# A second-layer mask added by GpSimd, head pairs in the third layer, and a new order of steps, in a four-layer graph kernel

## What is computed

```
x = layernorm(x + L0(x, adj))    # additive attention, leaky relu, softmax masked where adj == 0
x = layernorm(x + L1(x, adj))    # logits Ax^T + Ay + x M x^T, leaky relu, masked where adj <= 0, softmax, elu
x = layernorm(x + L2(x, adj))    # four heads of 32, masked where adj == 0 and off the diagonal, relu
x = layernorm(x + L3(x, adj))    # relation 1: onehot(adj) @ ((xW + b) * sigmoid(xWg + bg)), relu
```

## Time and profile before

| | us |
|---|---|
| median of 3 runs | 483.58 |
| the profiled execution, its own time | 484.45 |
| its span in the profile | 482.7 |
| TensorE matmul busy in the span | 451.3 (93%) |
| VectorE, ScalarE, GpSimd busy | 421.6, 418.1, 308.0 |

### The profile page before, as it was taken

How to read it: one execution, slowest core, us unless ns; L and a number is a source line. 1 busy time by engine, 2 the same in 40 slices (tenths; PEclk the granted TensorE clock), 3 DMA queues, 4 the chain that set the end, 5 groups by cost and what they waited for, 6 DMA issues and landing times. The chain is left out here.

```text
span 482.7 us, 13808 instructions
## 1 busy us (share of the span) xinstructions
PE 451.3 (93%) x3785; PEld 387.5 (80%) x3785; DVE 421.6 (87%) x1637; ACT 418.1 (87%) x1233; POOL 308.0 (64%) x671
## 2 busy tenths in 40 slices
PE   5878899999999999999999999999999999998862
PEld 5666787888889988888888988888888889886642
DVE  4478999999999999999999999999999999878662
ACT  3468999999999999999999999999999999988720
POOL 1245446787767667688767777777776777765441
PEclk9999999999999999999999999999999999999995
DMA  6443233334443333333344433333443321120011
GB/s 203 107 110 67 43 70 80 82 77 98 96 101 97 84 74 75 91 94 91 98 99 100 96 73 78 76 97 87 98 97 87 70 46 34 35 45 24 23 33 46
DMA packets 59942, 38.39 MB, mean 80 GB/s; under 512 B 11225, under 2 KB 55897, under 8 KB 59866
## 3 DMA queue, kind: packets, MB, share of 16 engines
q1 hardware_dynamic: 59866, 37.50, 32.1%
HBM read 25.24 MB, written 8.45 MB: 70 GB/s over the span
## 5 line engine op out<-in xcount | busy, mean ns | idle before, releaser
L1271 POOL TENSOR_SCALAR x<-y,minus_mean,rstd 128x128 f32<-128x128 f32 x244 | 121.7, 508 | 21.8 <-issue 19.4
L839 ACT ACTIVATE p<-p,nmax 128x256 f32<-128x256 f32 x256 | 127.2, 512 | 0.6 <-DVE nmax L1044 0.6
L1246 POOL TENSOR_SCALAR ve<-stats 128x2 f32<-128x2 f32 x128 | 30.6, 239 | 134.6 <-DVE stats L948 129.6
L1253 POOL TENSOR_TENSOR rstd<-ve,minus_half 128x2 f32<-128x2 f32 x128 | 104.3, 815 | 0.0
L1044 DVE CUSTOM_DVE_ANT_0 p<-ps,neg 128x256 f32<-128x256 f32 x256 | 90.8, 421 | 13.2 <-PE ps L607 13.2
L848 ACT COPY p2T<-ps 128x512 f32<-128x512 f32 x128 | 72.8, 607 | 0.1
L618 PE MATMUL ps<-ident,p 128*128 128x128 f32 x512 | 66.9, 273 | 1.5 <-issue 1.1
L618 PEld LDWEIGHTS ps<-ident,p 128*128 128x128 f32 x512 | 57.9, 141 | 2.8 <-issue 2.2
L948 DVE BATCH_NORM_STATS2 stats<-y 128x6 f32<-128x256 f32 x128 | 54.0, 422 | 1.4
L839 ACT ACTIVATION_READ_ACCUMULATOR p<-p,nmax 128x1 f32 x256 | 51.8, 202 | 0.0
L752 ACT COPY xT<-ps 128x256 f32<-128x256 f32 x96 | 36.4, 379 | 15.8 <-PE ps L479 15.7
(11 more groups left out here) (134 smaller groups left out, 1114.8 us busy)
## 6 DMA issues: line engine op xcount, KB each, us to landing
adj_in<-in_adj_dram SPq DMA_DIRECT2D x32, 256.0 KB, 4.3
s2row<-s_rows SPq DMA_DIRECT2D x29, 256.0 KB, 4.0
xT<-in_xT_dram SPq DMA_DIRECT2D x32, 128.0 KB, 4.3
x_in<-in_x_dram SPq DMA_DIRECT2D x32, 128.0 KB, 5.3
x_aside<-x SPq DMA_DIRECT2D x32, 128.0 KB, 3.6
out_dram<-x SPq DMA_DIRECT2D x32, 128.0 KB, 6.3
rs_row<-rs_turned SPq DMA_DIRECT2D x58, 64.0 KB
s_rows<-xw SPq DMA_DIRECT2D x29, 2.0 KB, 4.5
```

Of the source, the lines that this page charges most:

```text
L839: last = nc.scalar.activation(p2(n)[:, k, a, :], p2(n)[:, k, a, :], ACT.Exp, bias=nmax2(n)[:, k, a:a + 1], scale=-1.0, accum_out=sum2(n)[: ...
L1253: nc.gpsimd.tensor_tensor(rstd[layer](n), ve[layer](n), minus_half[:, :], ALU.pow)\
L1271: last = nc.gpsimd.tensor_scalar(dst[:, k, 0:D], y_t[layer](n)[:, k, :], minus_mean[layer](n)[:, k:k + 1], rstd[layer](n)[:, k:k + 1], ALU ...
```

## The change

Five things are changed together.

1. **L1 mask.** `relu1` now writes relu(z) times 4. A new GpSimd step `rmask1` adds the mask (now -9e15 / 0.2) to it. `e1` reads z from PSUM and this tile, and scales by -0.2. `lk1` is gone. The bank of `z1` is released by `e1` rather than by `lk1`.
2. **Head pairs in L2.** `e2`, `exp2` and `pT2` work on a row tile and a pair of heads, with semaphores for each pair. The number of instructions that compute is the same. Two banks of `sc2` are released when the first pair is read.
3. **Weights.** ACT issues the loads of `l1_w` and `l3_w` at its start; SP issues `l2_w`, `bias_rows` and `bo_row`, and does so ahead of the first `xT`.
4. **The end.** SP reads the flag before it waits for the last stores. The flag's three steps are moved forward. Some semaphores are shared to make room.
5. **Order.** Every place in `PLAN` is new, and `xT0` has four buffers instead of two.

```diff
-    "sc2": [("a", "e2a_ready", "e2b_ready")] * HEADS,
+    "sc2": [("a", f"e2a{a // 2}_ready", f"e2b{a // 2}_ready") for a in range(HEADS)],
...
-    "z1": [("b", "leaky_ready")],
+    "z1": [("b", "e1_ready")],
...
-    "tensor": [("proj0", 7293), ("s2_rows", 9289), ("prep_a", 9914), ("prep_c", 10981), ("pT0", 11117),
+    "tensor": [("proj0", 7882), ("s2_rows", 8921), ("prep_a", 9172), ("pT0", 11350), ("prep_c", 11355),
...
-            (l1_w[:, :], t["l1_w"]), (l2_w[:, :], t["l2_w"]), (l3_w[:, :], t["l3_w"]),
+            (l2_w[:, :], t["l2_w"]),
...
+        act_loads = [(l1_w[:, :], t["l1_w"]), (l3_w[:, :], t["l3_w"])]
...
+            flag = flag_value(sp)
             for s in range(RING["x4"]):
                 sp.wait_ge(sem(f"stored{s}"), 16 * len(range(s, B, RING["x4"])))
...
-            with if_relations(sp):
+            with sp.If(flag != 0):
...
-            def pT2(k, j, n):
+            def pT2(k, pair, n):
...
-                pe.wait_ge(sem(f"p_ready2{'ab'[k]}"), n + 1)
-                for a in range(HEADS):
-                    last = pe.transpose(o[:, a * P:(a + 1) * P], p2(n)[:, k, a, j * P:(j + 1) * P], ident[:, :])
+                pe.wait_ge(sem(f"p_ready2{'ab'[k]}{pair}"), n + 1)
+                for a in range(2):
+                    for j in range(T):
+                        last = pe.transpose(o[:, (a * T + j) * P:(a * T + j + 1) * P],
+                                            p2(n)[:, k, 2 * pair + a, j * P:(j + 1) * P], ident[:, :])
...
-                nc.scalar.activation(relu(n).rearrange("p t n -> p (t n)"), bank("z1", n), ACT.Copy,
-                                     scale=SLOPE).then_inc(sem("relu_ready"), 1)
+                nc.scalar.activation(relu(n).rearrange("p t n -> p (t n)"), bank("z1", n), ACT.Relu,
+                                     scale=(1.0 - SLOPE) / SLOPE).then_inc(sem("relu_ready"), 1)
...
-            def lk1(n):
...
             def e1(n):
-                dve.wait_ge(sem("leaky_ready"), n + 1)
-                dve.wait_ge(sem("neg1_ready"), n + 1)
+                dve.wait_ge(sem("rmask_ready"), n + 1)
                 free(dve, "p1", n, "pT_ps1")
-                for k in range(T):
-                    last = nc.vector.tensor_tensor_reduce(p1(n)[:, k, :], relu(n)[:, k, :], neg1(n)[:, k, :],
-                                                          -1.0, HIGHEST, ALU.add, ALU.min, nmax1(n)[:, k:k + 1])
+                o = bank("z1", n)
+                for k in range(T):
+                    last = nc.vector.tensor_tensor_reduce(p1(n)[:, k, :], o[:, k * N:(k + 1) * N], relu(n)[:, k, :],
+                                                          -SLOPE, HIGHEST, ALU.add, ALU.min, nmax1(n)[:, k:k + 1])
...
+            def rmask1(n):
+                pool.wait_ge(sem("neg1_ready"), n + 1)
+                pool.wait_ge(sem("relu_ready"), n + 1)
+                nc.gpsimd.tensor_tensor(relu(n), relu(n), neg1(n), ALU.add).then_inc(sem("rmask_ready"), 1)
```

More of the change, by code:

```diff
@@ L26 @@
 PLAN = {
-    "sync": [("ld_xT", 5924), ("ld_w", 7384), ("ld_adj", 7643), ("s2_out", 7682), ("s2_in", 8068), ("ld_x", 9856),
-        ("rs_in", 14874), ("aside", 17166), ("store", 18875)],
[5 rows of a table removed]
-        ("flag", 24911)],
-    "scalar": [("c_proj0", 7629), ("c_s2", 9333), ("c_prep_a", 9758), ("exp0", 10865), ("c_prep_c", 10970),
-        ("c_pT0", 11102), ("c_prep_d", 11926), ("c_xT1", 12167), ("c_tT", 12280), ("c_prep_b", 12346),
[12 rows of a table removed]
+    "sync": [("ld_w", -5093), ("ld_xT", 5803), ("ld_adj", 7317), ("s2_out", 8417), ("s2_in", 8928), ("ld_x", 9412),
+        ("rs_in", 15164), ("aside", 16727), ("store", 19522)],
[5 rows of a table added]
+        ("flag", 15769)],
+    "scalar": [("c_proj0", 8057), ("c_s2", 9237), ("c_prep_a", 10886), ("exp0", 11179), ("c_pT0", 11325),
+        ("c_prep_c", 11483), ("c_prep_b", 11609), ("c_prep_d", 11760), ("c_xT1", 12179), ("c_tT", 12195),
[9 rows of a table added]
+        ("flag_b", 15926), ("flag_a", 15780)],
+    "gpsimd": [("var0", 11818), ("rsq0", 11976), ("norm0", 12052), ("neg2", 12054), ("rmask1", 12530),
+        ("var1", 13523), ("rsq1", 13554), ("norm1", 13669), ("var2", 16156), ("rsq2", 16377), ("norm2", 16445),
+        ("var3", 18688), ("rsq3", 18724), ("norm3", 19112)],
 }
 RING = {
[1 row of a table removed]
[1 row of a table added]
     "x1": 3, "xT1": 2, "tT": 2, "xw1": 3, "relu": 2, "p1": 2, "p1T": 2, "h": 2, "hexp": 2,
@@ L317, in build, with flag_value @@
         rel_biases = ((t["L3_gnn_b_fwd"], t["L3_gnn_bg_fwd"]), (t["L3_gnn_b_bwd"], t["L3_gnn_bg_bwd"]))
+        def flag_value(engine):
+            engine.wait_ge(sem("flag_ready"), 1)
+            return engine.value_load(excess_flag[0:1, 0:1], min_val=0, max_val=1)
         def if_relations(engine):
-            engine.wait_ge(sem("flag_ready"), 1)
-            flag = engine.value_load(excess_flag[0:1, 0:1], min_val=0, max_val=1)
-            return engine.If(flag != 0)
+            return engine.If(flag_value(engine) != 0)
         wait_registers = {}
@@ L610, in sc2 @@
                             last.then_inc(sem("sc_ps"), 1)
-            def pT2(k, j, n):
-                step = f"pT2{'ab'[k]}{j}"
+            def pT2(k, pair, n):
+                step = f"pT2{'ab'[k]}{pair}"
                 o = bank(step, n)
                 bank_free(pe, step, n)
-                pe.wait_ge(sem(f"p_ready2{'ab'[k]}"), n + 1)
-                for a in range(HEADS):
-                    last = pe.transpose(o[:, a * P:(a + 1) * P], p2(n)[:, k, a, j * P:(j + 1) * P], ident[:, :])
+                pe.wait_ge(sem(f"p_ready2{'ab'[k]}{pair}"), n + 1)
[3 more added lines that the diff above has]
+                                            p2(n)[:, k, 2 * pair + a, j * P:(j + 1) * P], ident[:, :])
                 last.then_inc(sem("pT_ps2" + step[3:]), 1)
@@ L668, in relations @@
                                      start=True, stop=True)
-                last.then_inc(sem("rel_setup_pe"), 1)
-                pe.wait_ge(sem("rel_setup_sb"), 1)
+                last.then_inc(sem("setup_pe"), 1)
+                pe.wait_ge(sem("weights_ready"), 2)
                 with pe.Fori(0, B) as g:
-                    pe.wait_ge(sem("rel_adj_f_ready"), g + 1)
+                    pe.wait_ge(sem("rel_dve"), 3 * g + 1)
                     for j in range(T):
@@ L720, in setup @@
             def setup():
+                for dst, src in act_loads:
+                    act.dma_start(dst, src).then_inc(sem("weights_loaded"), 16)
                 act.wait_ge(sem("setup_pe"), 2)
@@ L832, in c_v2, with exp2 @@
                     .then_inc(sem("v_sb"), 1)
-            def exp2(k, n):
-                half = "ab"[k]
+            def exp2(k, pair, n):
+                half = f"{'ab'[k]}{pair}"
                 act.wait_ge(sem(f"e2{half}_ready"), n + 1)
                 free(act, "small", n, "rsum2_ready")
-                for a in range(HEADS):
+                for a in (2 * pair, 2 * pair + 1):
                     last = nc.scalar.activation(p2(n)[:, k, a, :], p2(n)[:, k, a, :], ACT.Exp,
@@ L842, in exp2, with c_pT2 @@
                 last.then_inc(sem(f"p_ready2{half}"), 1)
-            def c_pT2(k, j, n):
-                half = f"{'ab'[k]}{j}"
+            def c_pT2(k, pair, n):
+                half = f"{'ab'[k]}{pair}"
                 act.wait_ge(sem("pT_ps2" + half), n + 1)
                 free(act, "p2T", n, "agg_ps2", HEADS)
-                nc.scalar.copy(p2T(n)[:, :, j, k * P:(k + 1) * P],
-                               bank("pT2" + half, n).rearrange("p (h i) -> p h i", h=HEADS))\
+                nc.scalar.copy(p2T(n)[:, 2 * pair:2 * pair + 2, :, k * P:(k + 1) * P],
+                               bank("pT2" + half, n).rearrange("p (h j i) -> p h j i", h=2, j=T))\
                     .then_inc(sem("pT_sb2" + half), 1)
@@ L927, in masks @@
                 dve.wait_ge(sem(f"adj_loaded{n % RING['adj']}"), 16 * (n // RING["adj"]) + 16)
-                free(dve, "neg0", n, "e2a_ready")
-                free(dve, "neg0", n, "e2b_ready")
+                for part_of in ("a0", "a1", "b0", "b1"):
+                    free(dve, "neg0", n, f"e2{part_of}_ready")
                 nc.vector.tensor_scalar(neg0(n), adj_in(n), 0.0, NEG_INF, ALU.is_equal, ALU.mult)\
@@ L1034, in y1b, with e2 @@
                                                op0=ALU.min, op1=ALU.add).then_inc(sem("y1_ready"), 1)
-            def e2(k, n):
+            def e2(k, pair, n):
                 dve.wait_ge(sem("neg2_ready"), n + 1)
-                half = "ab"[k]
-                free(dve, "p2", n, f"pT_ps2{half}0")
-                free(dve, "p2", n, f"pT_ps2{half}1")
+                half = f"{'ab'[k]}{pair}"
+                free(dve, "p2", n, f"pT_ps2{half}")
                 free(dve, "small", n, f"p_ready2{half}")
-                for a in range(HEADS):
+                for a in (2 * pair, 2 * pair + 1):
                     dve.wait_ge(sem("sc_ps"), n * HEADS + a + 1)
@@ L1049, in r2 @@
```

(8 more changed lines are left out.)

41 lines of the change are left out of this document (19 added, 22 removed), and 31 rows, old and new, of tables (PLAN, RING).

## The result

The changed kernel takes **515.16 us** (median of 4 runs, 514.01 to 516.96) against 483.64 for the kernel before in the same session: ratio 1.0634, 95% interval 1.0607 to 1.066. The direction was as predicted (slower), the size was not: 504 was forecast, and 515.16 lies 1.2 us above the range. The profiled execution took 515.01, with a span of 513.2, 30.5 more than before where +20.5 was forecast.

What follows compares the result with a forecast made beforehand. PE's gapless instruction string was taken as the bound. Terms 2.1 + 3.5 + 17.4 + 3.3 + 0.6 - 2.0 - 4.4 = +20.5 on a span of 482.7 gave 503.2, hence 504 us, 8-in-10 range 492 to 514.

Steps and rivals of the forecast that it cites:

- the change of PE's shape: `agg2` and `sc2` now stand apart, so a graph has four changes of shape instead of three: +0.09 us a graph.
- the filling: Stretch from the start to the first `sc2`, bounded by the chain of the first graphs: +2.1 us.
- What bounds: In the middle, PE instructions run without a gap, 13.46 us a graph; relief on other engines is worth nothing there.
- The rival that DVE or ACT bounds: DVE's pace sets PE's string, so `lk1`'s 0.69 us come back in 25 periods: about 465 us, chance 6%.
- The gap on PE: Largest term: `tT` directly behind `xT1` waits for ACT's copy, so PE stands still 0.74 us in every graph.
- the 0.83 forecast: Added time per graph in the middle: 0.74 of standing still plus 0.09 for shape, making 14.29 us from 13.46.
- the first four periods: Four periods after the first `sc2`, whose chain holds the GpSimd addition and PE's standing still: +3.5 us.
- The mask: Dropping `lk1` saves DVE 0.69 us a graph, worth 0 in the middle; GpSimd's addition takes 1.4 us.
- The layout: One period's steps laid out on all engines: nothing else late, by 0.6 us or more; next bound near 15 us.
- the -1.0 of the start: At the start, `pT0` of graph 0 no longer stands behind `prep_c`: -1.0 us, with 1.5 of doubt both ways.
- The three that I had: Before the first `sc2`: addition for `lk1` +0.7; `agg1` behind `xT1` and `tT` +1.0; `norm1` behind the addition +1.6.
- Draining: Period 30 +0.6, period 31 -2.0; after the last `sc2` -4.4 us, of which the early flag read saves about 0.8.

Runs made afterwards that it cites:

- 1: Changed kernel with `tT` one step later on PE, behind `agg1`: 489.42 us, ratio 1.0091.
- 8: Changed kernel's code in the old order with layer two's mask back on DVE; head pairs, loads by ACT and early flag stay: 482.1 us, ratio 0.9939.
- 2: Kernel before with `tT` directly behind `xT1` on PE, `c_tT` left in its place on ACT: 551.41 us, ratio 1.1379.
- 3: Kernel before with `tT` directly behind `xT1` on PE and `c_tT` directly behind `c_xT1` on ACT: 521.9 us, ratio 1.0759.
- 4: Kernel before with `agg2` moved ahead of `qk2`, away from `sc2`: 516.23 us, ratio 1.0641.
- 7: Changed kernel's whole code, mask on GpSimd, with the old order of steps; only `rmask1` and the flag keep new places: 502.76 us, ratio 1.0372.
- 5: Kernel before with `xT3` placed between `agg2` and `sc2`: 492.06 us, ratio 1.015.
- 10: Changed kernel in its own order with the mask back on DVE (`lk1` ahead of `e1`, no `rmask1`): 519.31 us, ratio 1.0712.
- 6: Changed kernel with all five weight loads on SP behind the first inputs, as before: 515.0 us, ratio 1.0623.
- 9: Changed kernel's code in the old order, mask on GpSimd, with `xT2` and `c_xT2` one step later (behind `pT2a0` on PE): 504.28 us, ratio 1.0397.
- 11: Changed kernel's code in the old order, mask on DVE, flag steps placed as before; head pairs and loads by ACT left: 484.15 us, ratio 0.9987.
- 12: Changed kernel's code in the old order, mask on DVE, all weight loads on SP; head pairs and early flag left: 482.79 us, ratio 0.9958.

## Why the prediction was wrong in size

The direction and the mechanism of the largest term were right. Two steps failed: the change of PE's shape, put at 0.09 us a graph, is 0.25 and has a refill of 0.07 beside it that was put at nothing; and the filling, put at +2.1 us, is +6.5.

**What bounds** (a string of PE instructions without a gap; in the changed kernel the same string with one gap): right. 1 and 8 have it again, and in 2, 3, 4 and 7 each gap on PE showed in the time. The rival that DVE or ACT bounds, with the rule by the share of weight loads, is refuted in the same runs: in the changed kernel's middle that share is 248.41 of 304.80, 81%, below ACT's 89% and DVE's 87%, and yet the time moved with PE's stalls by one number of the table.

**The gap on PE**, 0.74: the place, the pair and the size were right. From `xT1` to `tT` 0.99 is 0.72 of waiting, 0.06 of leaving `sc2`'s shape and 0.22 of work. Missed was the refill of 0.07 in `tT` itself. It stood in the trace that I used: in the filling of the kernel before `tT` starts at 22.89 and the next step at 23.40.

**One more change of PE's shape**, 0.09: this is the step that failed in the middle. I counted only the way in, once. Experiments 1, 4 and 5 show the way out as well, 0.10 behind `agg2` and 0.06 behind `sc2`; that makes 0.25. In the kernel before `sc2` was followed by `rs_rows`, which paid nothing (0.11 there), so its way out could not be seen; and of the three changes that I counted only the one into `agg2` had a price. Together 0.72 + 0.07 + 0.25 = 1.04 a graph against the 0.83 forecast: over 21 graphs 21.8 (22.0 measured) and not 17.4, over the four behind them 4.2 and not 3.3. In the first four periods +4.9 was measured and +3.5 forecast; taking the gap out gives 4.0 of it back (1), and how the other 0.9 divides is open.

**The mask**: DVE's relief "hidden behind PE: 0" was right for the old order; in the new one it gives about 0.1 us a graph (10). That is no part of the miss: the 1.04 is measured with the relief in it. The addition was put at 1.4 and takes 1.16:

```profile
L1251 POOL TENSOR_TENSOR relu<-relu,neg 128x512 f32<-128x512 f32 x32 | 37.1, 1158 | 6.6 <-ACT relu L818 4.6
```

The layout held: it found 0.6 us of slack for `norm1` ahead of `xT2` and 0.8 for `e1` ahead of `xT3`, which takes `z1`'s accumulator, and PE waits for neither. What I had not asked is what the new order was needed for: in the old one `xT2` takes that accumulator, and `e1` is late for it (7).

**Filling**, +2.1 forecast, +6.5 measured: this step failed too, by 4.4, and mostly on a term that was not in the sum. The granted clock was 0.91 up to the first `sc2` (1.00 before). PE's timeline of the changed kernel:

```profile
21.94 0.41 PE L485 MATMUL ps<-ident,x 128*128 128x128 f32 x2 [1.00 <-POOL x L1280]
...
24.39 2.04 PE L579 MATMUL ps<-xT,tT 128*128 128x256 f32 x4
26.22 1.68 PE L504 MATMUL ps<-xw,p0T 128*128 128x129 f32 x8
...
34.53 1.93 PE L504 MATMUL ps<-xw,p1T 128*128 128x129 f32 x8
```

`xT1` of graph 0 starts as early as before (21.94, 21.93 in the earlier trace rows), so the -1.0 of the start was not there, and with early inputs it would have been 0.3 sooner (6). Then `z1` takes 2.04 and `agg1` 1.93 where their kind take 1.03 and 1.05, at a granted clock of 0.53 from 24 to 26 us and 0.59 from 34 to 36: that is mostly the lower of the two levels, 1.2 GHz and not 2.4. By their starts the two lose 1.8 us on the chain. `proj0` and `pT1` ahead of the first `sc2` lose 0.7 more to it (6). So 2.5 us are the clock, which was not in my sum. `e1` stands behind `y0` and `b0` of the next graph on DVE, 1.0: missed too. The three that I had are near: the addition for `lk1` 0.5 (0.7), `agg1` behind `xT1` and `tT` 1.1 (1.0), `norm1` behind the addition on GpSimd 1.2 (1.6). These are differences of starts in the two traces, and with 0.2 of small ones they add up to 6.5; none of them was tested alone, only the loads were (6).

The lower level shows ahead of the first `sc2` in all four traces of the new order (the changed kernel, 1, 6 and 10). In the old order it shows there in 3, 4, 7, 8 and 9, and not in 2, 5, 11, 12 and the kernel before. What the engine did before it fell doesn't tell the two apart: from 20 to 24 us PE was busy 2.19 of 4 us in the changed kernel, and 2.47 of 4 in the kernel before, where the clock stayed full. Four traces against ten are few, and why the clock falls I leave open.

**Draining**: periods 30 and 31 were right within 0.3. Behind the last `sc2`, -6.0 and not -4.4: `agg3` of the last graph starts 2.8 sooner, not 3.6; it takes 1.13 and not 2.04, since the granted clock was 1.00 there and 0.53 from 472 to 474 us in the kernel before, which was not in my sum:

```profile
506.86 1.13 PE L667 MATMUL ps<-vals,eq 128*128 128x128 f32 x8 [0.98 <-DVE vals L1124]
```

and the flag is worth 2.3, not 0.8 (the last `norm3` ends 2.3 us ahead of the span's end, and 4.6 before; see 11).

In sum the net error of 10.0 us is +4.4 in the filling to the first `sc2`, +6.9 in the 29 periods behind it, +0.3 in the last two and -1.6 at the end. Without the 2.5 of the lower clock in the filling the time would, by an estimate from these, have been 512.7 and inside the range, with the error of the string still in it: that the miss shows is in part bad luck. What is shown by experiment is the gap (1, 3), the prices of the shapes (1, 4, 5), the mask's two faces (7, 8, 10) and the early computing of the flag (11); the split of the filling, the refill and the read of the flag are read from traces, not tested alone.

## What to carry to other kernels

When one engine runs without a gap, as PE here, each pair "write, copy by another engine, read" on it needs work in between: 0.7 to 0.9 us here. Without it that much is lost in every round; a table of places should be read for such pairs first. Before an operation goes to another engine, ask who frees the buffer that it used to free, and who takes it next. And move a step together with the step that empties its accumulator: 2 and 3 differ by 30 us through that alone.

## What was not expected of the hardware

- A change between 128-row steps and those of 32 rows or columns is paid twice: 0.09 us in the last record ahead of it, and 0.06 (128 columns) or 0.10 (256 columns) in the first one behind it. The Trainium skill (TensorEngine Tiling (Array Packing), Key Properties) says that a change of tiling mode drains TensorE; the trace agrees, with 0.15 to 0.19 for the pair, but not for every change: from `agg2` (32 columns) straight into `sc2` (32 rows), and from `sc2` into `rs_rows` (8 columns), none shows.
- After a stall of 0.7 us the first step of two records with 256 columns takes 0.07 more (0.51 for 0.44, in the changed kernel and in 3).
- The granted clock differs from one execution to the next, and the time with it. In the traces of 8 and 11, whose filling is the same program, it was 0.59 and 1.00 around 24 us. Among the twelve executions of 11, 483.02 us at a mean clock of 0.991, 486.05 at 0.983. A single time of this kernel can't show half a per cent.
